# Softmax maxima of a two-head self attention: units of 512 token keys, the context's keys four query tiles to a bank, two units in every step

## What is computed

```
n   = layernorm(x)                                   # (2, 1024, 256)
q   = layer_norm(n) @ Wq                             # 8 heads of 64
k,v = split([layer_norm(ctx), layer_norm(n)] @ Wkv)  # 77 + 1024 = 1101 keys
q, k = l2norm(q) * q_scale, l2norm(k) * k_scale      # per head
sim  = q @ k.T * 8.0, masked context keys at -max
x   += layer_norm(softmax(sim) @ v @ Wo)
```

## Time and profile before

| what | value |
|---|---|
| runs (us) | 3022.64, 3035.03, 3035.06; median 3035.03 |
| the profiled execution's own time | 3037.68 us |
| its span in the trace | 3035.7 us |
| busy over the span | TensorE 2299.9 us (76%), VectorE 1425.4 (47%), ScalarE 1093.3 (36%), GpSimd 542.5 (18%) |
| stage `heads0` in the trace | about 179 to 640 us |
| mean granted clock of TensorE | 0.847 of full speed |

### The profile page before, as it was taken

One profiled execution on the slowest core, in us unless ns is written; L12 is line 12 of the kernel. 1 busy time (PEld: TensorE's weight loads), 2 busy tenths in 40 slices (PEclk: granted clock), 3 DMA queues, 4 the chain that ended last, 5 costly groups with the idle time before them and its releaser, 6 DMA issues. The chain is left out here.

```text
span 3035.7 us, 38003 instructions
## 1 busy us (share of the span) xinstructions
PE 2299.9 (76%) x12297; PEld 1336.9 (44%) x12298; DVE 1425.4 (47%) x2551; ACT 1093.3 (36%) x2264; POOL 542.5 (18%) x467
## 2 busy tenths in 40 slices
PE   4989899973285876799998289994947999482587
PEld 2423233242174343233334179982327999231354
DVE  4666666535513545787771510003641000448565
ACT  3413333421032351366665234432513444151111
POOL 0203344340042004000000022220002222103011
PEclk9979999985586887699999589996868999685699
DMA  1000000001052005243420466642045664200001
GB/s 56 1 1 8 12 12 8 12 21 55 28 195 89 1 13 143 24 50 36 56 30 6 140 205 205 195 141 72 1 132 193 204 196 156 69 1 29 7 14 35
DMA packets 145703, 216.35 MB, mean 71 GB/s; under 512 B 39840, under 2 KB 101980, under 8 KB 145580
## 3 DMA queue, kind: packets, MB, share of 16 engines
q1 hardware_dynamic: 135884, 188.27, 22.9%
q0 software_dynamic: 9696, 26.49, 2.3%
HBM read 182.00 MB, written 30.15 MB: 70 GB/s over the span
## 5 line engine op out<-in xcount | busy, mean ns | idle before, releaser
L2799 PE MATMUL experts_up_ps<-experts_rowT,experts_w 128*128 128x128 f32 x2864 | 342.1, 278 | 0.0
L1647 DVE TENSOR_REDUCE heads_part_max<-heads_shared_ps 128x2 f32<-128x1024 f32 x256 | 300.0, 1220 | 75.7 <-PE heads_shared_ps L1564 75.7
L2799 PEld LDWEIGHTS experts_up_ps<-experts_rowT,experts_w 128*128 128x128 f32 x2864 | 334.1, 195 | 0.2
L1631 ACT ACTIVATE heads_probs<-heads_score_ps 128x512 f32<-128x512 f32 x512 | 266.3, 603 | 176.6 <-PE heads_score_ps L1586 176.6
L2949 DVE TENSOR_TENSOR experts_y<-experts_down_ps,experts_b_now 128x256 f32<-128x256 f32 x78 | 33.1, 425 | 556.1 <-PE experts_down_ps L2809 556.1
L1382 DVE TENSOR_REDUCE heads_part_max<-heads_shared_ps 128x1 f32<-128x367 f32 x384 | 181.1, 530 | 128.3 <-PE heads_shared_ps L1272 127.8
L2859 ACT ACTIVATE experts_hT<-experts_up_ps,experts_b_now 128x128 f32<-128x128 f32 x624 | 208.1, 367 | 83.0 <-PE experts_up_ps L2799 66.0
L1586 PE MATMUL heads_score_ps<-heads_q,heads_k 66*128 66x512 f32 x512 | 190.5, 455 | 31.5 <-ACT heads_probs L1631 27.3
L1363 ACT ACTIVATE heads_probs<-heads_score_ps 128x1024 f32<-128x1024 f32 x128 | 131.1, 1024 | 218.2 <-PE heads_score_ps L1299 215.7
L2809 PE MATMUL experts_down_ps<-moe_w,experts_hT 128*128 x808 | 184.4, 379 | 0.0
L2748 POOL DMA_INDIRECT y_dram<-experts_y,experts_index x101 | 99.7, 987 | 455.2 <-DVE experts_y L2949 410.2
(11 more groups left out here) (557 smaller groups left out, 3512.3 us busy)
## 6 DMA issues: line engine op xcount, KB each, us to landing
experts_w<-in_L_ffn_W SPq DMA_DIRECT2D x39, 1024.0 KB
experts_w<-in_L_ffn_w SPq DMA_DIRECT2D x39, 1024.0 KB
experts_w<-in_L_ffn_W SPq DMA_DIRECT2D x23, 512.0 KB
core_xT<-y_dram SPq DMA_DIRECT2D x20, 512.0 KB, 4.9
experts_b_now<-in_L_ffn_b SPq DMA_DIRECT2D x78, 128.0 KB
heads_q<-l_queries SPq DMA_DIRECT2D x32, 256.0 KB, 11.9
heads_k<-l_keys SPq DMA_DIRECT2D x32, 256.0 KB, 14.2
l1f_w<-in_L_ffn_W SPq DMA_DIRECT2D x8, 1024.0 KB, 11.8
```

What stands on the lines that cost most here:

```text
L1631: act.activation(probs[:, t % SLOTS_OF_PROBS, r, :], score_ps[:, i % RING, :], ACT.Exp, scale=SC).then_inc(exp_done, 1)
L1647: dve.tensor_reduce(part_max[:, g % 2, 2 * pair:2 * pair + 2, s, x], two, AX.X, ALU.max).then_inc(shared_read, 1)
L2799: done = pe.matmul(up_ps[:, f % 4, 0:SLOT], w1_sb[:, u, c, f * P:(f + 1) * P], rowT[:, u % 2, c, :], start=(c == 0), stop=(c == DC - 1))
```

## The change

A unit for tokens now takes 512 of the 1024 token keys (`TOKENS` = 2), a full bank. The 77 keys of the context get units of their own: four matmuls of 77 columns each put four query tiles of one head side by side into one bank, and one reduction gives four maxima (`EACH` = 4, `CONTEXTS` = 2). A pair has 8 x 2 x 2 = 32 token units and then 2 x 2 = 4 context units, 36 in place of 48. Every one of the 18 steps takes two units, steps 3 and 12 too, where they stand behind WEIGH. `LEAD` is 6. The context units of pair g + 1 fall into steps 13 and 14; TURN stays in step 15, behind two units. The three partial maxima per query stay three (two token halves and the context).

```
@@ -1107,16 +1107,17 @@
     HALVES = S // 512
     PER = HALVES * CHUNKS
     STEPS = PAIRS * PER
-    THIRDS = 3
-    PIECE = KEYS // THIRDS
-    UNITS = BT * THIRDS * 2
+    TOKENS = S // 512
+    CONTEXTS = 2
+    EACH = BT // CONTEXTS
+    UNITS = 2 * (BT * TOKENS + CONTEXTS)
     SLOTS_OF_PROBS, BANKS = 5, 3
     LAST = KEYS - (CHUNKS - 1) * P
     BY_POOL = [1, 3, 5, 6, 7]
     BY_VECTOR = [0, 2, 4, CHUNKS - 1]
     POOL_ADDS, VECTOR_ADDS = len(BY_POOL) - 1, len(BY_VECTOR)
-    NO_UNITS, TURN_AT, WEIGH_AT = (3, 12), 15, {3: 1, 12: 0}
-    LEAD = 9
+    TURN_AT, WEIGH_AT = 15, {3: 1, 12: 0}
+    LEAD = 3 * 2
     PEAK, TURN, WEIGH = "peak", "turn", "weigh"
 
     def place(g):
@@ -1126,7 +1127,10 @@
         return t // PER, t % PER // CHUNKS, t % CHUNKS
 
 
-    units = [(PEAK, g, s, x, r) for g in range(PAIRS) for s in range(BT) for x in range(THIRDS) for r in range(2)]
+    units = []
+    for g in range(PAIRS):
+        units += [(PEAK, g, s, x, r) for s in range(BT) for x in range(TOKENS) for r in range(2)]
+        units += [(PEAK, g, i, TOKENS, r) for i in range(CONTEXTS) for r in range(2)]
     work_at = {t: [] for t in range(-1, STEPS + 4)}
     work_at[-1] = units[0:UNITS] + [(TURN, 0)] + units[UNITS:UNITS + LEAD]
     left = units[UNITS + LEAD:]
@@ -1134,9 +1138,9 @@
         g, s = t // PER, t % PER
         if s in WEIGH_AT and 0 <= HALVES * g + WEIGH_AT[s] - (s == 3) * HALVES < HALVES * PAIRS:
             work_at[t].append((WEIGH, HALVES * g + WEIGH_AT[s] - (s == 3) * HALVES))
-        if s not in NO_UNITS and t < STEPS:
-            work_at[t] += left[0:3]
-            left = left[3:]
+        if t < STEPS:
+            work_at[t] += left[0:2]
+            left = left[2:]
         if s == TURN_AT and g + 1 < PAIRS:
             work_at[t].append((TURN, g + 1))
     number, reads, count, seen = {}, [], 0, {"vector": 0, "scalar": 0}
@@ -1151,7 +1155,7 @@
     with Stage(nc, name) as st:
         ones = st.sb("ones", [P, P])
         ones2 = st.sb("ones2", [P, P], F32R)
-        part_max = st.sb("part_max", [P, 2, 2, BT, THIRDS])
+        part_max = st.sb("part_max", [P, 2, 2, BT, TOKENS + 1])
         minus_max = st.sb("minus_max", [P, 2 * BT])
         max_parts = st.sb("max_parts", [2 * BT, 2, P], F32R)
         max_rows = st.sb("max_rows", [P, 2, S], F32R)
@@ -1268,8 +1272,15 @@
                     _, g, s, x, r = item
                     b, c = place(g)
                     rows = slice(HW * r, HW * (r + 1))
+                    if x == TOKENS:
+                        for i in range(EACH):
+                            at = b * S + (s * EACH + i) * P
+                            done = pe.matmul(bank[:, i * KV:(i + 1) * KV], q16[rows, c, at:at + P], k16[rows, c, b, S:KEYS],
+                                             start=True, stop=True, tile_position=(HW * r, 0))
+                        done.then_inc(shared_done, 1)
+                        return
                     at = b * S + s * P
-                    pe.matmul(bank[:, 0:PIECE], q16[rows, c, at:at + P], k16[rows, c, b, x * PIECE:(x + 1) * PIECE],
+                    pe.matmul(bank, q16[rows, c, at:at + P], k16[rows, c, b, x * 512:(x + 1) * 512],
                               start=True, stop=True, tile_position=(HW * r, 0)).then_inc(shared_done, 1)
                 elif item[0] == TURN:
                     pe.wait_ge(minus_ready, item[1] + 1)
@@ -1379,8 +1390,13 @@
                     dve.wait_ge(shared_done, used + 1)
                     if g >= 2 and (s, x, r) == (0, 0, 0):
                         dve.wait_ge(minus_ready, g - 1)
-                    dve.tensor_reduce(part_max[:, g % 2, r, s, x:x + 1], bank[:, 0:PIECE], AX.X, ALU.max).then_inc(shared_read, 1)
-                    if (s, x, r) == (BT - 1, THIRDS - 1, 1):
+                    if x == TOKENS:
+                        dve.tensor_reduce(part_max[:, g % 2, r, s * EACH:(s + 1) * EACH, x],
+                                          bank[:, 0:EACH * KV].rearrange("p (s k) -> p s k", k=KV), AX.X,
+                                          ALU.max).then_inc(shared_read, 1)
+                    else:
+                        dve.tensor_reduce(part_max[:, g % 2, r, s, x:x + 1], bank, AX.X, ALU.max).then_inc(shared_read, 1)
+                    if (s, x, r) == (CONTEXTS - 1, TOKENS, 1):
                         dve.wait_ge(shared_read, n)
                         if g:
                             dve.wait_ge(shared_done, number[TURN, g - 1] + 1)
```

## The result

The changed kernel took 3048.44 us (median; 3037.64 to 3058.66), the kernel before 3034.49 us in the same measurement (3022.64 to 3048.38), 16 runs each: a ratio of 1.005, 95% interval 1.0035 to 1.0066, so 14 us slower. The forecast was 3033.5 us and no change, with a range from 3016 to 3048. The profiled execution of after took 3048.9 us, 11.2 more than that of before.

A forecast was written before the change was run, and what follows sets the result against it. TensorE's own work was taken as the bound where it runs without a pause, elsewhere its pauses. Work 6.3 us less and slow starts 4.8 us more gave 1.5 us less, 3033.5 us against the median 3035.03, range 3016 to 3048.

The forecast's parts named there:

- The clock at seven starts: First steps of a pair after the wait for loads: 1.55 us lost each, 10.9 in place of 6.1, 4.8 more.
- Ordinary steps: Steps 0 to 2, 4 to 6, 9 to 11: 0.10 us less each, 0.9 a pair, to 2.51 us.
- Steps 3 and 12: Steps that now carry units behind WEIGH: a slot and two gaps more, 0.41 us each, 0.8 us a pair.
- Step 7: Step whose units wait for reads behind `add(4)`: 0.5 us a pair saved, to near 2.9 us.
- Context units: Steps 13 and 14: eight matmuls of 77 columns take 0.3 us, so step 13 costs as much as before.
- Ahead of step 0: Reductions before the first step, where VectorE is the bound: 20.7 against 21.4 us, 0.7 us saved once.
- The chain from u: From step 14's units (u) to the next pair's scores: `add(13)` ends where it did, shorter reads save 0.15 us.
- The wait at TURN: TensorE's wait ahead of TURN: its 13.0 us go but do not come off the time, since the loads end the chain.
- The clock stays down: Rival, chance 0.14: every pair start costs 4.54 us, 25.7 us more, less 6.3, giving 3054.
- The add that wins the race: Rival, chance 0.18: `add(13)` begins before GpSimd's add, 1.7 us shorter seven times, 11.9 us, giving 3021.6.
- The clock holds: Rival, chance 0.1: no pair start is slow, 12.4 us less, giving 3022.6.
- The two heads do not overlap: Rival, chance 0.03: at 512 columns, 0.21 us more in 18 steps of seven pairs, 27 us more.

The follow-up runs named there:

- a_split: The changed kernel with the wait at TURN put back, for the first read of step 15: 3034.14 us, ratio to before 0.9993.
- a_add14: The changed kernel with VectorE's `add(13)` put ahead of the two reads of the context units in step 14: 3025.8 us, ratio to before 0.9961.
- a_fill: The changed kernel with 16 unread matmuls added ahead of the wait for the loads at pairs 1 to 7: 3031.42 us, ratio to before 0.9987.
- b_loads: The kernel before with SyncE issuing the four loads of the maxima ahead of the store and spread of `invert`: 3020.24 us, ratio 0.9953.

## Why the prediction failed

**The step that failed** is "The clock at seven starts", where it says "A wait of some 4.5 us is nearest to the 4.23 us one, so 1.55: 7 x 1.55 = 10.9 us". The mechanism was right (the wait moves to the loads, and each start is slowed), but this term was mis-sized: it measured 21.9 us in place of 10.9, as four of the seven starts cost 4.1 to 4.5. That is 11.0 us of the miss of 15.5 (a forecast of 1.5 less against 14 more); the work came out 0.9 better (7.2 against 6.3), and the remaining 5.4 lie outside the account and are not explained.

I chose the nearest row by the length of the wait alone. The row of 4.23 us was the start of the last pair, the only one without units around it, and in after that start again waited 4.24 us and cost 1.6. The prediction also says "The other five changes look like the one at 314.56", as if the clock had held there. It had fallen there too, at TURN, 7 us earlier, as the first of the two step 16 rows above shows for one of the five. The one change of before in which nothing fell at TURN is the one to pair 3, and its start cost 4.54 after only 2.71 us; in after every change is of that kind. With units and a wait of 3.64 or 3.67 us a start cost 1.4; with 3.86 and longer, 4.1 to 4.5. But the 2.71 us of before, and 3.2 us lost after 1.96 us in a_split, do not fit one rule by the wait's length, so what decides between the two prices stays open. The bounds of the earlier trace rows, 0 to 4.54 a start, held the truth; the upper one deserved more weight in the range.

**The other steps, one by one.** Ordinary steps: 2.51 us, as forecast. Steps 3 and 12: 4.00 (forecast 3.93). Step 7: 2.91 (2.9). Context units: eight matmuls in 0.25 us to the next instruction (354.29 to 354.54), against 0.3. The Trainium skill's time for a weight load (TensorE: Matmul & The Clock Gate, section LDWEIGHTS (loading the stationary operand)), taken eight times in a row, would have made that an estimated 0.85 us. The trace has 95 ns for one load of these units (107 by the Trainium skill), but they overlap: seven of the eight take 0.19 us together. So the row of eight does not occur, here as in the earlier trace rows. Ahead of step 0: 0.7 us saved, as forecast. The chain from u: `add(13)` begins 0.04 us behind GpSimd's add, the very 0.04 of the forecast, and ends 1.08 us after it (that so small a margin came out was partly luck: the estimate had VectorE's reads begin at u + 0.35, and they began at u + 0.33); the first score came 0.2 us sooner from u (0.15). The wait at TURN is gone and gave nothing, and the wait for the loads is 3.6 to 4.8 us (4.5).

**The rivals.** "The clock stays down" is what happened at four starts of seven: 15.8 us more over all seven, where the rival had 25.7. The measured mean of 3.1 us a start lies between the rival's turning point of 1.8 and the 3.9 that it gave for 15 us; it deserved more than 0.14. "The add that wins the race" lost by 0.04 us in all seven pairs, and a_add14 gives its price, 1.7 us a start. The Trainium skill (SBUF — State Buffer, section SBUF: two separate sides) says that the first of the two holds the shared ports for its whole instruction; the trace agrees, as VectorE's add took 3.40 us when it began second, ending 1.08 us behind GpSimd's, and 1.21 when it ran ahead. "The clock holds" is a_fill, made by hand. "The two heads do not overlap" is excluded by the 2.51 us step, which would have been 0.21 us longer.

## What to carry to other kernels

A wait that is removed gives nothing if a later wait of the same chain ends last, and it can cost: the slow stretch that had followed the first of two pauses, where it was hidden, now followed the last one, and that took more than the change saved. Before pricing a start, read the granted clock behind every pause of the chain, also where a slow stretch costs nothing: a start that looks free may owe it to an earlier pause. And look at what stands ahead of the last transfer in its queue: here moving four loads ahead of a round trip that nobody hurried for was worth 48 us with the new units, over three times what the change cost.

## What the runs showed of the hardware

- Behind the pause at a start two cases occurred in after and nothing between them: 3.9 us at a granted clock near 0.6 (starts at 257.79, 428.53 and 598.59) and some 10 us near 0.5 (the other four). Waits of 3.67 and 3.86 us fell on different sides; the cause is open. In a_split and a_add14 there are starts between the two, which cost 3.2 us.
- Behind the pauses of 2.14 to 2.17 us at TURN, step 16 was slow at five of six changes in before (granted clock 0.60 to 0.72); in b_loads, with the same pauses, at two of six (4.2 us in place of 2.61).
- Sixteen matmuls without use and a wait without need made a kernel 17 and 14 us faster.
- A few hundredths of a us in the order of VectorE and GpSimd decide which of the two is held. In the middle of pair 1 VectorE's add of the 77 context keys meets GpSimd's scaling of the queries. In after GpSimd begins 0.04 us ahead and VectorE takes 2.31 us; in a_add14 VectorE begins 0.01 us ahead, takes 1.21 us, and GpSimd takes 2.33 in place of 1.26. First after, then a_add14:

```profile
286.41 1.26 POOL L1249 TENSOR_TENSOR self_qT<-self_qT,heads_spread 128x512 f32<-128x512 f32 x1 [2.52 <-DMA heads_spread<-heads_inverse_rows]
286.45 2.31 DVE L1434 TENSOR_TENSOR core_xT<-core_xT,heads_probs 77x1024 f32<-77x1024 f32 x1
```

```profile
287.28 1.21 DVE L1434 TENSOR_TENSOR core_xT<-core_xT,heads_probs 77x1024 f32<-77x1024 f32 x1
287.29 2.33 POOL L1249 TENSOR_TENSOR self_qT<-self_qT,heads_spread 128x512 f32<-128x512 f32 x1 [2.58 <-DMA heads_spread<-heads_inverse_rows]
```
